# An attention core with one transpose per shift and two head groups per output bank, the scan's inner products first, and a new step order

## What is computed

```python
x = x + 0.5 * ffn(layernorm(x))
x = x + mamba(layernorm(x))
x = x + 0.5 * ffn(layernorm(x))

def ffn(x):                       # 16 heads of 8 channels, 4 experts
    h = causal_conv3(layernorm(x) * ln1_w + ln1_b)
    q, k, v = rope(split(h @ attn_w))
    p = softmax(causal(q @ k.T / sqrt(8)))
    x = x + (p @ v) @ proj_w
    h = layernorm(x) * ln2_w + ln2_b
    e = argmax(h @ router_w)      # one expert for each token
    return x + (silu(gate(h, e)) * value(h, e)) @ expert_proj[e]

def mamba(x):                     # 4 heads of 64, state of 64
    z, xBC, dt = split(x @ W_in); xs, B, C = silu(conv4(xBC))
    h[t] = exp(dt[t] * A) * h[t-1] + dt[t] * xs[t] * B[t]
    y = h[t] @ C[t] + D * xs
    h = x + rmsnorm(y * silu(z)) @ W_out
    return h + silu(rmsnorm(h) @ w1 + b1) @ w2 + b2
```

## Time and profile before

| | |
|---|---|
| median of 3 runs | 1715.63 us (1712.78 to 1719.43) |
| span of the profiled execution | 1727.8 us |
| PE busy, share | 1426.8 us, 83% |
| DVE | 1173.5 us, 68% |
| ACT | 800.8 us, 46% |
| POOL | 400.0 us, 23% |
| mean granted clock of PE | 0.886 |

### The profile page before, as it was taken

One profiled execution on the slowest core, in us unless ns is written; L12 is line 12 of the kernel. 1 busy time (PEld: TensorE's weight loads), 2 busy tenths in 40 slices (PEclk: granted clock), 3 DMA queues, 4 the chain that ended last, 5 costly groups with the idle time before them and its releaser, 6 DMA issues.

```text
span 1727.8 us, 30410 instructions
## 1 busy us (share of the span) xinstructions
PE 1426.8 (83%) x11328; PEld 747.2 (43%) x11328; DVE 1173.5 (68%) x2803; ACT 800.8 (46%) x1266; POOL 400.0 (23%) x406
## 2 busy tenths in 40 slices
PE   1567779979978989898998989899899888796946
PEld 1223444544433545344454545354455444443423
DVE  4556585687685787668767779778786677565622
ACT  1243443644544565354553566455555454263522
POOL 3000132232332131412123031513133214211120
PEclk8687878979988999898897999899999899797978
DMA  6220200303020030122101221121202103002110
GB/s 188 36 33 25 48 1 18 55 1 53 20 31 24 8 59 19 36 38 45 27 19 34 40 47 20 48 41 31 38 13 53 49 1 55 23 2 54 31 35 23
DMA packets 75807, 61.43 MB, mean 36 GB/s; under 512 B 6800, under 2 KB 71824, under 8 KB 75664
## 3 DMA queue, kind: packets, MB, share of 16 engines
q1 hardware_dynamic: 70704, 50.31, 14.8%
q0 software_dynamic: 4096, 8.40, 1.6%
q10 hardware_dynamic: 864, 0.79, 0.4%
HBM read 19.23 MB, written 14.55 MB: 20 GB/s over the span
## 4 chain that ended last, share of the span: by engine, by line
PE 42%; DVE 14%; issue 6%; SPq 3%; DMA 3%; ACT 3%; POOL 2%; POOLq 0%; DVEq 0%; ACTq 0%
PE wring L747 7%; PE wring L554 5%; PE obank L600 5%; PE wring L752 4%; DVE mx L1307 4%; PE aring L615 4%; SPq L463 3%; PE aring L657 3%; PE aring L640 2%; PE wring L760 2%; PE aring L580 2%; DMA stq<-shiftT 2%; DVE conv L1443 1%; PE wring L862 1%; PE wring L766 1%
## 5 line engine op out<-in xcount | busy, mean ns | idle before, releaser
L943 ACT ACTIVATE prob_mem<-aring 128x1024 f32<-128x1024 f32 x320 | 324.9, 1021 | 185.5 <-PE aring L657 172.0
L1307 DVE TENSOR_REDUCE mx<-aring 128x2 f32<-128x1024 f32 (+2 forms) x384 | 317.6, 861 | 128.8 <-PE aring L640 117.6
L615 PE MATMUL aring<-ramps,spots 64*128 64x128 bf16 (+1 forms) x2560 | 179.9, 220 | 88.3 <-DVE mx L1307 26.4
L747 PE MATMUL wring<-wv,hb 128*128 x448 | 238.1, 637 | 7.8 <-ACT hb L980 4.9
L615 PEld LDWEIGHTS aring<-ramps,spots 64*128 64x128 bf16 x2560 | 84.5, 97 | 307.6 <-issue 193.1
L600 PE MATMUL obank<-prob_mem,vx 128*9 128x512 f32 (+3 forms) x2048 | 193.3, 477 | 15.0 <-ACT prob_mem L943 9.1
L1418 DVE SCALAR_TENSOR_TENSOR yv<-yv,wring 128x512 f32<-128x512 f32 x112 | 76.6, 684 | 99.4 <-ACT yv L985 98.5
L657 PE MATMUL aring<-stq,stk 50*128 50x384 bf16 (+3 forms) x1024 | 135.0, 323 | 0.0
L640 PE MATMUL aring<-stk,stq 48*128 48x512 bf16 (+3 forms) x1024 | 134.4, 324 | 0.0
L752 PEld LDWEIGHTS wring<-ep,yaT 128*128 128x128 f32 x896 | 112.7, 194 | 44.1 <-issue 43.6
L752 PE MATMUL wring<-ep,yaT 128*128 x896 | 126.9, 285 | 5.7 <-ACT yaT L877 3.5
(11 more groups left out here) (212 smaller groups left out, 2377.3 us busy)
## 6 DMA issues: line engine op xcount, KB each, us to landing
hb<-hd SPq DMA_DIRECT2D x16, 448.0 KB
stq<-high SPq DMA_DIRECT2D x96, 64.0 KB
stk<-high SPq DMA_DIRECT2D x90, 64.0 KB
stq<-mid SPq DMA_DIRECT2D x64, 64.0 KB
od<-ob SPq DMA_DIRECT2D x16, 256.0 KB, 2.3
stk<-mid SPq DMA_DIRECT2D x60, 64.0 KB
od<-ob SPq DMA_DIRECT2D x16, 192.0 KB, 2.0
x<-in_x SPq DMA_DIRECT2D x8, 256.0 KB, 2.8
```

The lines of the kernel that those rows point to most:

```text
L615: pe.matmul(dst, spots[rows, 2 * by_key + part, :], ramp, start=(part == 0), stop=False, skip_group_check=True)
L747: last = pe.matmul(ring[:], hTd[:, u * P:(u + 1) * P], wv[:, expert[u], o:o + DFF], start=True, stop=True)
L943: act.activation(prob_mem[:, k], ring[:], ACT.Exp, scale=float(HD) ** -0.5).then_inc(freed, 1)
L1307: last = dve.tensor_reduce(mx[:, j, h0 + q:h0 + q + 3:2], ring[:, :, c:c + w], AX_X, ALU.max)
```

## The change

Five things are changed.

- The shift tile is laid out with the four token blocks innermost, so that PE transposes its 32 columns at once, in place of four times 8. `shiftT` has 32 rows of 128 in place of 8 of 512, and the DMAs take 16 rows each.
- `vx` holds for each pair of heads three blocks of 9 columns: one head, zeros, the other head. A product takes the 18 columns that begin at 0 or at 9, so that group `2k` adds to the first 9 rows and zeros to the other 9, and group `2k+1` the other way round. Two groups share one output bank, which is copied, transposed and divided once for both. The copy of the values into `vx` is in two halves.
- `Y0` and `Y1` do all products within chunks first, then those with the carried state.
- `e_hT` uses the memory of `yT`.
- `ORDER` is another string, with 32 core steps fewer.

```diff
-        if g + 1 < GROUPS:
-            at.append((TILES * (g + 2) + BEHIND + 2.6, ("back", g)))
+        if g % 2 and g + 1 < GROUPS:
+            at.append((TILES * (g + 2) + BEHIND + 2.6, ("back", g // 2)))
...
 ORDER = (
-    "00000000000011111111001110111111101111111111110111111111001111101111121122202112212111100116110114114444440444"
+    "00000000000111111110111111111111101101111101011111111100111001110111211121212026211210101111114114114444444114"
...
-    "4441411411144114115114411441455111111122222522264444444444444444444444544444444555"
+    "44444444444444444445654444444444444444444454454545554"
...
-        shift = sb("shift", [P, 4, GROUP * SHIFTS], BF16)
-        shiftT = sb("shiftT", [GROUP * SHIFTS, T], BF16)
-        vx = [sb(f"vx{k}", [P, 4, HEADS, HD + 1]) for k in range(2)]
+        shift = sb("shift", [P, GROUP * SHIFTS, 4], BF16)
+        shiftT = sb("shiftT", [GROUP * SHIFTS * 4, P], BF16)
+        vx = [sb(f"vx{k}", [P, 4, MIDDLE, 3 * VW]) for k in range(2)]
...
-                                         shiftT[GROUP * piece:GROUP * (piece + 1), :]).then_inc(s["a_shifted"], 16)
+                                         shiftT[4 * GROUP * piece:4 * GROUP * (piece + 1), :]).then_inc(s["a_shifted"], 16)
...
-                    if part == 0 and n * GROUPS + g > 0:
-                        pe.wait_ge(s["a_osb"], n * GROUPS + g)
+                    if part == 0 and g % 2 == 0 and n * OUTS + g // 2 > 0:
+                        pe.wait_ge(s["a_osb"], n * OUTS + g // 2)
+                    side = g % 2
...
-                        last = pe.matmul(obank[32 * hl:32 * hl + HD + 1, 512 - w:512], vx[n % 2][:, kb, GROUP * g + hl, :],
-                                         prob_mem[:, k, a, c:c + w], start=(part == 0), stop=(part == 2), skip_group_check=True)
+                        last = pe.matmul(obank[32 * hl:32 * hl + 2 * VW, 512 - w:512],
+                                         vx[n % 2][:, kb, GROUP * (g // 2) + hl, VW * side:VW * side + 2 * VW],
+                                         prob_mem[:, k, a, c:c + w], start=(part == 0 and side == 0),
+                                         stop=(part == 2 and side == 1), skip_group_check=True)
...
-                        dst = flat[0:GROUP * SHIFTS, 0:T // 2].bitcast(BF16)
-                        last = transpose4(lambda j: dst[:, j * P:(j + 1) * P], lambda j: shift[:, j, :], identb[:])
+                        last = pe.transpose(flat[0:GROUP * SHIFTS * 4, 0:P // 2].bitcast(BF16), shift[:].rearrange("p c j -> p (c j)"),
+                                            identb[:])
...
                         for j in range(4):
                             if kind == "Y0":
                                 pe.wait_ge(s["m_Lg"], 4 * i + j + 1)
-                                if j > 0:
-                                    pe.wait_ge(s["m_Ce"], 3 * i + j)
-                            last = outputs(ring, int(kind == "Y1"), j)
+                            within(ring, int(kind == "Y1"), j)
+                        for j in range(1, 4):
+                            if kind == "Y0":
+                                pe.wait_ge(s["m_Ce"], 3 * i + j)
+                            last = carried(ring, int(kind == "Y1"), j)
...
-                        copy(shiftT[:], ring[0:GROUP * SHIFTS, 0:T // 2].bitcast(BF16)).then_inc(s["a_shiftT"], 1)
+                        copy(shiftT[:], ring[0:GROUP * SHIFTS * 4, 0:P // 2].bitcast(BF16)).then_inc(s["a_shiftT"], 1)
...
-                        if k == 1 and g > 0:
-                            copy_out(g - 1)
+                        if k == 1 and g > 0 and g % 2 == 0:
+                            copy_out(g // 2 - 1)
...
-                    last = dve.tensor_tensor(y[:, j, 32 * g:32 * g + 32].rearrange("p (h d) -> p h d", d=HD), o[:, j, :, 0:HD],
-                                             rden[:, j, :].unsqueeze(2).to_broadcast([P, GROUP, HD]), ALU.mult)
+                    last = dve.tensor_tensor(y[:, j, 64 * k:64 * k + 64].rearrange("p (a h d) -> p a h d", a=2, d=HD), o[:, j, :, :, 0:HD],
+                                             rden[:, j].unsqueeze(3).to_broadcast([P, GROUP, 2, HD]), ALU.mult)
```

More of the change, by code:

```diff
@@ L34 @@
 GROUPS = HEADS // GROUP
+OUTS = GROUPS // 2
+VW = HD + 1
+MIDDLE = HEADS // 2
+HALF = HEADS // 2
 HALF = 64
@@ L85, in core_steps @@
         at.append((TILES * g + TILES - 0.9, ("shift", g)))
-        if g + 1 < GROUPS:
-            at.append((TILES * (g + 2) + BEHIND + 2.6, ("back", g)))
+        if g % 2 and g + 1 < GROUPS:
+            at.append((TILES * (g + 2) + BEHIND + 2.6, ("back", g // 2)))
     return [step for _, step in sorted(at)] + [("pv_last",)]
-BACK = [("back", GROUPS - 1), ("yT",), ("proj",), ("e_stats",), ("e_norm",), ("e_hT",), ("logits",), ("rank",)]
+BACK = [("back", OUTS - 1), ("yT",), ("proj",), ("e_stats",), ("e_norm",), ("e_hT",), ("logits",), ("rank",)]
 def expert_steps():
@@ new lines @@
+    "33411034434411444441144403444444114343113444444134455114133113053113531313111331303333313111133111311321321312"
+    "12333231320312113123310363311033034041144404113114403401144443411454441444444141143415044310134103311353035313"
+    "13103331333313311133113111311110133231123311312112313331211333121102361332113311110131011411311134144411403444"
+    "11104110441411144124411442442544412421145432411542411233033113151613301131110341131431104311031144341104441141"
+    "34144441331434111431531444131331142144411244244121413553312131231211331151231136113111331331011343011441104311"
@@ L177 @@
+    "44444444444444444445654444444444444444454454545554"
 )
@@ L313, in build_program @@
         e_hn = u
-        e_hT = sb("e_hT", [P, T])
+        e_hT = yT
         lmax = sb("lmax", [P, 4])
@@ L538, in _ @@
                 sp.dma_start(dst[:], src).then_inc(s["weights_loaded"], 16)
[L539 removed]
+            sp.wait_ge(s["setup_pool"], 18)
             for k in range(2):
@@ L677, in back @@
                     flat, _, _ = w_slot(t)
-                    reads = {("yT",): [("back", GROUPS - 1)], ("proj",): [("yT",)], ("logits",): [("e_hT",)]}.get(task, [])
+                    reads = {("yT",): [("back", OUTS - 1)], ("proj",): [("yT",)], ("logits",): [("e_hT",)]}.get(task, [])
                     w_used(pe, *[a_fill[n][read] for read in reads], fill=t)
                     if kind == "back":
-                        pe.wait_ge(s["a_osb"], n * GROUPS + GROUPS)
+                        pe.wait_ge(s["a_osb"], n * OUTS + OUTS)
                         last = transpose4(lambda j: flat[:, j * P:(j + 1) * P], lambda j: osb[:, j * P:(j + 1) * P], ident[:])
@@ L760, in chunk, with within, carried @@
                     return pe.matmul(ring, w[:, n0:n0 + m], src[:], start=True, stop=True)
[L762 to L767, removed]
-                    if j > 0:
-                        for a, dst in enumerate(dsts):
-                            last = pe.matmul(dst, St[:, j, 2 * c + a, :], Ed[:, j, 2 * c + a, :], start=False, stop=True,
-                                             skip_group_check=True)
+                def within(bank, c, j):
+                    for a in range(2):
+                        last = pe.matmul(bank[MP * a:MP * a + MP, j * P:(j + 1) * P], Xd[j // 2][:, j % 2, 2 * c + a, :],
+                                         Ld[:, j, 2 * c + a, :], start=(j == 0), stop=False, skip_group_check=True)
+                    return last
+                def carried(bank, c, j):
+                    for a in range(2):
+                        last = pe.matmul(bank[MP * a:MP * a + MP, j * P:(j + 1) * P], St[:, j, 2 * c + a, :],
+                                         Ed[:, j, 2 * c + a, :], start=False, stop=(j == 3), skip_group_check=True)
                     return last
@@ L918, in core, with copy_out @@
             def core(n, row, half):
[L919 to L923, removed]
+                def copy_out(k):
+                    act.wait_ge(s["a_pv"], (n * GROUPS + 2 * k + 2) * len(PRODUCTS))
+                    if k > 0:
+                        a_used(act, n, ("back", k - 1))
                     elif n > 0:
-                        a_used(act, n - 1, ("back", GROUPS - 1))
+                        a_used(act, n - 1, ("back", OUTS - 1))
                     copy(osb[:], obank[:]).then_inc(s["a_osb"], 1)
@@ L1173, in _ @@
                 pool.memset(cpad[c][:, 0:3], 0.0).then_inc(s["setup_pool"], 1)
-            pool.memset(vx[0][:, :, :, HD:HD + 1], 1.0).then_inc(s["setup_pool"], 1)
-            pool.memset(vx[1][:, :, :, HD:HD + 1], 1.0).then_inc(s["setup_pool"], 1)
+            for k in range(2):
+                blocks = vx[k][:].rearrange("p j b w -> p (j b) w")
+                pool.memset(blocks[:, :, VW:2 * VW], 0.0).then_inc(s["setup_pool"], 1)
+                for side in range(2):
+                    first = 2 * VW * side + HD
+                    pool.memset(blocks[:, :, first:first + 1], 1.0).then_inc(s["setup_pool"], 1)
```

(14 more changed lines are left out.)

46 lines of the change are left out of this document (21 added, 25 removed).

## The result

The kernel after takes 1566.79 us (median of 4 runs, 1562.68 to 1570.68); the kernel before, on the same chip, 1714.20. The ratio is 0.9151, 95% interval 0.9111 to 0.9191: 147 us less. I had forecast 1667 and a range that ended at 1628. The sign was right; the gain is three times the sum.

The account below looks back on a forecast made before the run. PE was taken to bound the kernel. From the median 1715.6, 33 PE work + 3 waits + 14 last rows + 8 SP + 4 `rank` - 8 fronts = 54, less 5 for the ends, 49, gave 1667 us; range 1628 to 1702.

Parts of the forecast that it names:

- 33 us of PE work: Backs 19, shift transposes 10 and scan products 10 make 39 us less on PE, counted at 0.85.
- 3 of waits: Shorter way of the shift from ACT to `stq`, and half the `osb` waits gone: 3 us less, bounds 0 to 6.
- less 5 for the ends: Backs of the first and last rows, where PE waits anyway: 5 us taken off the gain.
- the scan's share: Products in Y0 and Y1 with fewer row changes: 0.6 us for each of 16 outputs, 10 us, bounds 0 to 10.
- The output loads with 18 columns: Wider weight loads of 2048 output products: taken as 0; rival in the open +23 us, 1690, chance 0.03.
- 15 were forecast: Behind the last core, experts fill the waits for normalised rows and `hb`: 15 us less.
- collisions on SP (-8): Shifts within 10 steps behind a batch of stack DMAs fall from 12 to 6: 8 us less waiting.
- `rank` (-4): In the new list `rank` stands directly behind `logits` nowhere, before three times: 4 us less.
- a give-back at the fronts (+8): Attention fronts' `hT` has under 10 PE steps over DVE's statistics in 10 of 15 cases, 5 before: 8 us lost.
- no help: A shift directly behind its last max tile in 7 of 64 groups, 6 before: no gain on the 47.1 us wait.
- the order packs much better: Rival: all steps stand anew, a further 0.3 of the middle's 171.8 us idle goes, 1615 us; chance 0.12.
- Core 15 gives 7 back: Last core keeps 20 filling steps of 31 and waits more for DVE and ACT: 7 us lost, bounds 2 to 12.

Follow-up runs that it names:

- e1: Kernel after (new operations) with the step list of before, less the 32 back steps that no longer exist: 1675.86 us, 0.9814 of before.
- e2: Kernel before (old operations) with the new step list, the 32 backs put back and one expert step three places earlier: 1591.67 us, 0.9322 of before.
- e9: Kernel after with 329 pairs of neighbouring list steps exchanged, each including an attention core step: 1693.75 us, +127 us against after.
- e10: Kernel after with 127 pairs of neighbouring list steps exchanged, none including an attention core step: 1628.65 us, +62 us against after.
- e5: Kernel before with 373 PE products for nothing added ahead of 50 waits of over 1 us, no step moved: 1682.94 us, 0.9804 of before.
- e8: Kernel after with the 22 expert steps that stand behind core 15 put back between its steps: 1589.51 us, +23 us against after.
- e7: Kernel after with 456 pairs of neighbouring list steps from different lanes exchanged by coin: 1752.85 us, +186 us against after.
- e12: Kernel after with 333 PE products for nothing added ahead of 39 waits of over 0.7 us: 1530.68 us, -36 us against after.

## Why the prediction was wrong

**What held.** The operations: the sum had 33 us of PE work and 3 of waits, less 5 for the ends, 31 in all; e1 measures 31 (23 to 40). So close a match is partly luck, since the scan's share of it measured 11 and 3. The output loads with 18 columns take 99 ns for 91; had they cost 23 us in the open, e1 would have gained 8, which its interval shuts out if the other terms are right. The shift copy fell from 579 to 258 ns, the division is 19.7 us in all, the shift's DMAs are no slower. Shift x64, `osb` x128 and `Y1` read as announced. Behind the last core, PE idles 14.3 us less; 15 were forecast. The split was other than forecast: the last `hb` is waited for 0.66 us and not 4 to 5, so other waits there are longer than I counted.

**What failed: the order's middle term.** I counted collisions on SP (-8), `rank` (-4) and a give-back at the fronts (+8), 4 us of gain, and put everything else in the middle at nothing. The middle's idle time fell by 52.7 us, and where all terms of the order came to 18 us, the list brought 115 (e2). PE's waits from 230 us to the end of the last core, columns as in the earlier trace rows, before and after:

```profile
PE wring L554 <- DVE shift L1318: 32.5, 23, 3.0
PE aring L615 <- DMA stq<-shiftT: 17.7, 5, 6.8
PE aring L615 <- DMA stk<-low: 9.5, 1, 9.5
...
PE wring L701 <- DVE pick L1360: 7.0, 5, 2.3
...
PE wring L554 <- DVE hn L1229: 2.6, 2, 2.0
```

```profile
PE wring L653 <- DVE shift L1337: 25.8, 22, 2.9
PE aring L622 <- DMA stk<-low: 15.5, 4, 5.8
...
PE aring L622 <- DMA stq<-shiftT: 6.6, 3, 3.2
...
PE wring L558 <- DVE hn L1243: 2.8, 1, 2.8
```

One by one:
- SP: PE's wait for the shift's DMA fell by 11.1 us (17.7 to 6.6); I had said 8.
- `rank`: PE's wait for its `pick` was 7.0 us in 5 waits and is gone; I had said 4.
- Fronts: the wait for `DVE hn` stayed as it was (2.6 and 2.8 us; the long ones, 17.2 and 14.5 us before, stand in the start). The give-back came one step later, at `stk<-low`: without the last core's own wait (9.51 before, 5.76 after) it rose from nothing to 9.7 us, where I had 8.
- Shift: 32.5 to 25.8, where I said "no help".

So the kinds that I counted moved about as forecast: 8 us of gain in place of 4. With the shift's 6.7 and the last core's 3.7 that is some 19 of the 52.7. The other 34 are many small waits that no count of mine covered. Exchanged pairs cost 0.39 us on average with a core step and 0.49 without (e9, e10), so a choice of a few kinds of pairs cannot be expected to give the sum for a list of 1920 steps.

**What was left out: the clock.** The text began with "PE both idles and works in part at the lower of its two levels", and no term followed. Idle time that goes takes lower-clock time with it, and the steps beside it get shorter: 30 to 35 us for the new list, as estimated above from e1, e2 and after. e5 shows that the clock does this by itself, with no wait shortened. The rival "the order packs much better" took 0.3 of the middle's idle time, 52 us, and the middle lost 52.7. The 0.3 came from no row, so the match is luck; with a clock term of 30 to 35 on top that rival would have said 1580 to 1585, for the 1567 measured. It was given 0.12, and priced at less than half of the list's 115.

**What was mis-sized in the tail.** "Core 15 gives 7 back" should have been near 0 (its idle time went from 5.0 to 7.6 us against before, and is 9.0 in e8), and the whole shift of the experts was worth 23 (e8), not 8. The wait before core 15 fell from 9.51 to 5.76, 3.7 in place of 6.

**The accounts of the 159 us between the two spans:** 32 of PE's busy time are the operations (e2 to after, 1370.7 to 1338.6), 56 the same instructions getting shorter (30 to 35 by the list, the rest by the profiled execution of before), 52.7 idle time of the middle, 14.3 of the tail, 4 elsewhere.

**What stays open.** That the new list is the better one is shown, that exchanges at random cost both alike, and which waits fell; which of its larger moves does it isn't. No run took the list in halves.

## What to carry to other kernels

Where every engine walks one written list, price a new list as a whole, with a range as wide as a shuffle of it moves the time (here 180 us), and not by counting a few kinds of neighbours. Give idle time of TensorE a price above one: from e1 to after each microsecond less idle took 0.40 of busy time with it; in e7 each one more added 0.66, in e8 0.35. And before shortening waits, try filling them: products for nothing ahead of 39 waits were worth some 36 us here (e12).

## What the runs showed of the hardware

- The same 11328 PE instructions took 1426.8, 1370.7 and (e5, without the added ones) 1360.2 us of busy time, at mean granted clocks of 0.886, 0.923 and 0.936, and of the first some is that execution's alone. A profile's busy time is not a sum of fixed lengths.
- Waits filled with 512-column bf16 products, whose results are overwritten, raised the mean granted clock: 0.936 in e5, where the runs of before beside it had at most 0.903, and 0.962 in e12 for 0.916 in after.
- Issuing a stack DMA holds ACT's own instructions about as long as SP's queue (six in 4.21 us, SP 1.27 for two): behind the six an exponential stood 4.41 us.
